# Edge weights moved from the gathered rows into the target marks in the streaming stage of a four-layer graph network

## The reference

```python
row, col = edge_index
h = gelu(concat([x[row], x[col]], -1) @ mlp_w1 + mlp_b1, approximate=False)
edge_weight = sigmoid(h @ mlp_w2 + mlp_b2)[:, 0]
row_f = concatenate([row, arange(n)]); col_f = concatenate([col, arange(n)])
ew_f = concatenate([edge_weight, ones(n)])
deg = segment_sum(ew_f, col_f, n)
dinv = where(deg > 0, rsqrt(deg), 0.0)
norm = dinv[row_f] * ew_f * dinv[col_f]
out = segment_sum((x @ conv_w)[row_f] * norm[:, None], col_f, n) + conv_b
```

## Time and profile before

| what | value |
|---|---|
| median of 3 runs | 4776.23 us (4770.1 to 4780.95) |
| span of the profiled execution, first to last instruction | 4768.7 us |
| its own time outside the span | not listed |
| mean granted TensorE clock | 0.831 |
| busy over the span: PE, DVE, ACT, POOL | 3392.9, 2341.6, 1316.9, 2458.3 us |
| streaming stage: row scaling on ACT (L1143), 784 | 239.6 us |
| streaming stage: target marks on DVE (L2370), 98 | 130.0 us, 1326 ns each |
| streaming stage: product and reduction on DVE (L2363, L2367), 98 each | 55.0 us and 55.0 us |
| streaming stage: segment sums on PE (L1451), 1552 seen | 208.6 us |
| streaming stage: spread on PE (L1655), 2352 | 78.0 us |

### The profile page before, as it was taken

One profiled execution on the slowest core, in us unless ns is written; L12 is line 12 of the kernel. 1 busy time (PEld: TensorE's weight loads), 2 busy tenths in 40 slices (PEclk: granted clock), 3 DMA queues, 4 the chain that ended last, 5 costly groups with the idle time before them and its releaser, 6 DMA issues.

```text
span 4768.7 us, 66594 instructions
## 1 busy us (share of the span) xinstructions
PE 3392.9 (71%) x22549; PEld 2236.1 (47%) x22549; DVE 2341.6 (49%) x5563; ACT 1316.9 (28%) x3113; POOL 2458.3 (52%) x2489
## 2 busy tenths in 40 slices
PE   3888888885676766774333333347777999999998
PEld 3554545553455544552222222236774555555554
DVE  6755555553566565663555555546773111111122
ACT  1233223322122222222444444436772000000000
POOL 3777777774777777775777777753230000000000
PEclk8999999997888888886555555558998999999999
DMA  3343344442333333334777777776776777777776
GB/s 106 105 125 120 121 134 133 130 124 94 91 99 95 99 103 100 99 90 115 197 199 200 200 200 199 197 207 231 267 264 245 279 276 281 280 277 280 291 295 224
DMA packets 506525, 855.10 MB, mean 179 GB/s; under 512 B 111339, under 2 KB 284439, under 8 KB 506180
## 3 DMA queue, kind: packets, MB, share of 16 engines
q1 hardware_dynamic: 338752, 542.03, 32.4%
q0 software_dynamic: 87808, 179.98, 14.9%
q10 hardware_dynamic: 79620, 128.70, 7.5%
HBM read 632.93 MB, written 217.55 MB: 178 GB/s over the span
## 4 chain that ended last, share of the span: by engine, by line
POOL 48%; PE 27%; issue 16%; DVE 4%; ACT 3%; DMA 1%; SPq 0%; DVEq 0%; ACTq 0%; POOLq 0%
POOL big L767 33%; POOL big L794 16%; PE psS L1774 11%; PE psA L1774 11%; ACT big L1143 2%; PE psS L1451 2%; PE ps L1720 1%; PE ps L1711 1%; DVE xn L2363 1%; PE psA L1655 1%; DVE wcol L2367 1%; DMA big<-in_src_dram 0%; PE ps L1644 0%; DMA big<-A_rows 0%; PE ps L1386 0%
## 5 line engine op out<-in xcount | busy, mean ns | idle before, releaser
L767 POOL DMA_INDIRECT big<-ht_rows,reli x784 | 790.7, 1009 | 275.4 <-issue 238.6
L767 POOL DMA_INDIRECT big<-xw_rows,srci x784 | 765.1, 976 | 308.7 <-issue 238.7
L794 POOL DMA_INDIRECT big<-axt_rows,srci x784 | 744.3, 949 | 264.1 <-issue 238.5
L1451 PE MATMUL psS<-big 128*128 128x128 f32 x3136 | 505.4, 329 | 310.6 <-DMA big<-ht_rows,reli 309.5
L1451 PEld LDWEIGHTS psS<-big 128*128 128x128 f32 x3136 | 473.8, 239 | 381.0 <-DMA big<-ht_rows,reli 346.7
L851 POOL TENSOR_TENSOR xsb<-xsb,l3b2r 128x896 f32<-128x896 f32 x6 | 12.5, 2078 | 1115.1 <-DMA xsb<-x_keep 1115.1
L1774 PE MATMUL psS<-big,xsb 128*128 128x448 f16 x1372 | 484.9, 353 | 18.6 <-DMA big<-A_rows 18.6
L1596 PE MATMUL ps<-identh,xsb 128*128 128x128 bf16 x784 | 101.4, 311 | 546.4 <-DVE xsb L2266 546.4
L1774 PE MATMUL psA<-big,xsb 128*128 128x448 f16 x1372 | 484.7, 353 | 0.0
L1774 PE MATMUL psS<-big,acc 128*128 128x448 f16 x1372 | 483.6, 352 | 0.0
L1774 PE MATMUL psA<-big,acc 128*128 128x448 f16 x1372 | 483.6, 352 | 0.0
(11 more groups left out here) (291 smaller groups left out, 5129.9 us busy)
## 6 DMA issues: line engine op xcount, KB each, us to landing
big<-A_rows SPq DMA_DIRECT2D x112, 2744.0 KB, 13.5
A_rows<-xsb ACTq DMA_DIRECT2D x196, 416.0 KB, 2.7
xg_rows<-big SPq DMA_DIRECT2D x98, 512.0 KB, 3.8
big<-xg_rows SPq DMA_DIRECT2D x98, 512.0 KB, 3.7
marks_rows<-big SPq DMA_DIRECT2D x98, 354.0 KB
big<-marks_rows SPq DMA_DIRECT2D x98, 354.0 KB, 4.6
big<-srcq_list SPq DMA_DIRECT2D x98, 256.0 KB
ht_rows<-big ACTq DMA_DIRECT2D x28, 512.0 KB
```

Source lines behind the costliest of these rows:

```text
L767: pool.indirect_dma_start(ring[g % len(ring)][:, j * D:(j + 1) * D], None, table[:, :], bass.IndirectOffsetOnAxis(ap=lists[:, g * TPG + j: ...
L794: pool.indirect_dma_start(wide[g % NS][:, j, :], None, axt_rows[:, :], bass.IndirectOffsetOnAxis(ap=srci[:, g * TPG + j:g * TPG + j + 1], ...
L1451: m = pe.matmul(psS[b][:, 0:P], rows[b][:, j * P:(j + 1) * P], marks[b][:, j * P:(j + 1) * P], start=(j == 0), stop=(j == TPG - 1))
```

## The change

Three things change, all in the streaming stage.
- DVE's target marks carry the weight. `row_marks` waits for the reduction of its own group (`e_w`) and then issues eight `tensor_scalar` instructions, one a tile, each 128 x 128 f32: the window's node numbers compared with the edge's target, and the result multiplied by the edge's weight. Both are per-partition scalars read from SBUF.
- ACT's `scale_rows` and the semaphore `e_scaled` are gone. ACT copies the sums of g - 1 in its turn g.
- PE spreads groups 0 and 1 first, and then in turn g the spread of g + 2 ahead of the sums of g. The sums no longer wait for `e_scaled`.

The change as a diff, with the branch that doesn't run (`more > 0`) left out:

```diff
             with act.If(more < 1):
 ...
                 for g in range(NG):
-                    scale_rows(g)
-                    if g >= 2:
-                        copy_sums(g - 2)
+                    if g:
+                        copy_sums(g - 1)
                     early_n3(g)
-                for g in range(NG - 2, NG):
-                    copy_sums(g)
+                copy_sums(NG - 1)
 ...
             with pe.If(more < 1):
-                spread_dinv(0, 0, 0, 0)
+                for g in range(2):
+                    spread_dinv(g, 0, g, 0)
                 for g in range(NG):
                     b, it = g % 2, g // 2
-                    if g + 1 < NG:
-                        spread_dinv(1 - b, (g + 1) // 2, (g + 1) % NS, (g + 1) // NS)
-                    pe.wait_ge(e_scaled, g + 3)
+                    if g + 2 < NG:
+                        spread_dinv(b, it + 1, (g + 2) % NS, (g + 2) // NS)
                     pe.wait_ge(r_oh[b], it + R2b.g0 + 1)
 ...
                 dve.wait_ge(e_prod[b], pair + 2)
-                dve.wait_ge(e_scaled, g + 1)
                 dve.tensor_reduce(wcol[:, b, :], prod[:, b, :].rearrange("p (j s) -> p j s", s=NB), AXX, ALU.add).then_inc(e_w, 1)
 
-            def row_marks(b, base, w, pair):
-                dve.tensor_tensor(tiles(marked[b]), iota[:, window(base, w)].unsqueeze(1).broadcast_to([P, TPG, P]),
-                                  columns(dstf, pair, b), ALU.is_equal).then_inc(r_oh[b], 1)
+            def row_marks(b, base, w, pair, g):
+                dve.wait_ge(e_w, g + 1)
+                for j in range(TPG):
+                    m = dve.tensor_scalar(marked[b][:, j * P:(j + 1) * P], iota[:, window(base, w)], column(dstf, pair, b, j),
+                                          wcol[:, b, j:j + 1], ALU.is_equal, ALU.mult)
+                m.then_inc(r_oh[b], 1)
```

More of the change, by code:

```diff
@@ L352, in gnn_program @@
         e_w = sem("e_w")
-        e_scaled = sem("e_scaled")
         rows_out = sem("rows_out")
@@ L884, in _ @@
             act.sem_inc(b_ev, 2)
-            act.sem_inc(e_scaled, 2)
             def setup_turn(c):
@@ L1135, in _ @@
             act.activation(droot[:, :], ps4[:, 0:NB], ACT.Sqrt, bias=onec[:, :]).then_inc(k_ready, 1)
[L1137 to L1144, removed]
             def turned_back(c):
@@ L1168, in _ @@
             with act.If(more > 0):
-                for g in range(NG):
-                    scale_rows(g)
                 summed(R2b)
@@ L1677, in _ @@
                         spread_dinv(b, pair, k, use)
-                        pe.wait_ge(e_scaled, body * BODY + n + 3)
                         segment_sums(both(back[k]), b, (pair + R2b.g0) * nwin, marked)
@@ L2401, in _ @@
                         edge_scales(b, pair, body * BODY + n, k)
-                        row_marks(b, base, 0, pair)
+                        row_marks(b, base, 0, pair, body * BODY + n)
                         add_sums(b, base, 0, q, q)
                         with dve.Fori(1, more + 1) as w:
-                            row_marks(b, base, w, pair)
+                            row_marks(b, base, w, pair, body * BODY + n)
                             add_sums(b, base, w, q + w, q)
@@ L2417, in _ @@
                     dve.wait_ge(r_seg[b], it + R2b.g0 + 1)
-                    row_marks(b, base, 0, it)
+                    row_marks(b, base, 0, it, g)
                     early_n3(g)
```

## The result

The changed kernel takes 4840.59 us (median of 4 runs, 4832.23 to 4845.88) against 4775.03 for the kernel before (4 runs): a ratio of 1.0132, with a 95% interval of 1.0118 to 1.0146. That is 66 us slower, where 8 us faster was forecast, and outside the range of 4746 to 4822. The profiled execution has a span of 4841.1 us against 4768.7.

What follows compares the result with a forecast made beforehand. A loop of latencies bounded the stage, then DVE would: 98 x 2.85 (279.3) + 55 chunk work + 23 collisions + 0.1 from 3234.14 gives 3591.5, 9 us earlier, 1 given back: 4768 us, range 4746 to 4822.

Steps and rivals of the forecast that it cites:

- The bound: Streaming stage: a loop of latencies before the change; after it DVE bounds, with a cycle of 2.85 us per group.
- The second scalar: Each of DVE's 784 marks: price bounded by 0 and 0.06 us, taken as 0; other end 46 us.
- Rival 1: DVE's 784 marks: the second scalar is paid, up to 0.06 us each, 4814 us in full; chance 0.25.
- The marks at one scalar: DVE's eight marks per group: 1.65 us to the next instruction's start, after the degree stage's compare.
- Reduction to first mark: DVE, each group: 0.60 us with the wait, 0.56 plus the 0.04 separating product and reduction.
- The addition: POOL's addition of sums (L834), each group: meets the last mark or next product, costs DVE nothing; other end 29 us.
- rival 2: DVE's marks: POOL's additions break into them, 0.3 us a group, time 4797 us; chance 0.12.
- The long POOL instructions: 21 in the stage, three a chunk, colliding with DVE's marks: up to 1.1 us each, 23 us, between 0 and 35.
- The register load: Window's base, between DVE's marks and next product: counted as hidden; exposed, 59 us at most.
- Chunk work: DVE normalises six chunks inside the stage: 9.2 us per chunk, 55 us, all on the path.
- The early spread: PE's spread two groups ahead: takes PE's order out of the loop; given no price of its own.
- rival 3: DVE's marks are cheap and transfers at 338 GB/s hold the cycle at 2.62 us: time 4723 us; chance 0.10.

Runs made afterwards that it cites:

- experiment 7: Changed kernel with POOL's addition of the sums cut from 128 to 8 columns: 4822.33 us, ratio to before 1.0111.
- experiment 6: Changed kernel with constant 1.0 as the marks' second scalar and the marks of a group behind the next group's product and reduction: 4760.07 us, ratio to before 0.9980.
- experiment 5: Changed kernel with POOL's 21 full-width instructions of the stage cut from 896 to 128 columns: 4812.23 us, ratio to before 1.0090.
- Experiment 2: Kernel before with only PE's spread two groups ahead, ACT's scaling and DVE's one marks instruction kept: 4717.01 us, ratio to before 0.9878.

## Why the prediction was wrong, point by point

- **The bound.** "DVE becomes the bound" held: 91% busy, no wait for PE after the start, PE waiting for the marks.
- **The second scalar, taken as 0.** This is the step that failed, and the largest term. Its upper bound, 0.06 us from the one-element instructions of the earlier trace rows, was the truth: 0.257 - 0.197. Over 784 marks that is 47 of the 77 us by which the stage passed the forecast. I chose between the ends by likeness to the earlier trace rows, and likeness spoke only of what those rows contain, which was one scalar. The rows that differed in a scalar, rows 6, gave the price. Rival 1 had mechanism, place and price; 0.25 was too little for it.
- **The marks at one scalar.** 1.65 us came from one group of the degree stage. The usual step there is 0.197, so eight take 1.58, and the term was 7 us too high. It hid part of the miss: 47 - 7 = the ledger's 40.
- **Reduction to first mark, taken as 0.60.** It took 0.77. I carried the 0.04 us gap of product to reduction over, where nothing lies between the wait and the instruction. Here a semaphore instruction and the window's register work do. 98 x 0.17 = 17 us, and no rival had it.
- **The addition, taken as 0 by its phase.** It starts 2.59 us behind the sums (2.55 forecast), so the clock of the argument was right. But the marks now run until 3.70 us and so lie across it. The term hung on the 2.85, and fell with it: 15 us in the ledger, 14 in the stage by experiment 7, half of rival 2's 29. It was not nothing at the short cycle either: in experiment 6 an addition that began inside the last mark cost 0.2 us. A mark that it enters is 0.24 to 0.29 us longer in an otherwise equal cycle (3.65 to 3.70 against 3.41). The exclusive lock of the Trainium skill (SBUF — State Buffer, SBUF: two separate sides) is what these rows look like: with the additions cut, the marks lengthened by 0.05 to 0.4 us fall from 65 to 2.
- **The long POOL instructions**, 23 us. Measured 29.6 in the marks' steps, and 24.8 of stage by experiment 5. Held roughly: 18 of 1.64 us each in place of 21 of 1.1.
- **The register load, taken as hidden.** Held: no gap between marks and product in quiet groups.
- **Chunk work, 55 us.** Held: 55.9.
- **The early spread.** I counted it as a link opened and gave it no price of its own. Experiment 2 shows that it was worth 59 us by itself, with every scaling left on ACT. The change added about 1.5 us per group to DVE, the engine that then limited it (eight marks for one 1.2, the wait 0.3), so its other half could use only about 10 of these 59 us. The prediction's opening had the key, "a loop of latencies" with no full engine; what it did not ask is what would be left of the loop if one link alone were cut.

The sum, 77 us: second scalar 47, less 7 for the marks' base, gap 17, additions 15, long instructions 7, and about 2 less over the small terms and by rounding. With the second scalar and the wait taken out (experiment 6) the stage is within 6 us of the forecast, in part because other terms cancel.

## What to carry to other kernels

A loop of latencies is opened by moving the producer earlier, and that should be priced alone before any work is moved: here it was worth 59 us, and about 12 more with the chunk work cut into short pieces. Where one instruction becomes many, every operand and every wait of the small one counts by its number, and a price bounded by "0 or what the first one costs" should be taken at the upper end unless a row shows two of them. An argument by phase holds only for the cycle that it was worked out with, so it needs redoing at the cycle of each rival.

## What the runs showed of the hardware that was not expected

- A second per-partition scalar read from memory costs a DVE `tensor_scalar` of 128 x 128 f32 about 60 ns: steps of 0.257 and 0.197 us with two and with one. That is what the first costs in the one-element instructions (0.20 against 0.14 us); marks without any were not run. The output's type, f32 or bf16, made no difference (280 and 281 ns).
- A wait of DVE for its own last result costs 0.03 to 0.04 us when the waiting instruction follows directly, and 0.21 when a semaphore instruction (21 ns) and a register instruction (52 ns) stand between them.
- A POOL instruction that starts among short DVE instructions holds the next one until it is done: behind one of 2.12 us, a mark begun 0.05 us later took 2.16 us instead of 0.34, and cost 1.83 us more than a usual step.
- The transfers reached 370 GB/s in a quiet stretch, at a DMA share of 1.01, where the kernel before had 338 at most in the rows shown. The ceiling that I used for rival 3 was too low.
